# Three phase borders rearranged and the angle products of a random-feature attention stacked to 128 rows

## The reference, cut to what matters

```python
xn = layernorm(x)
x = x + features_attention_and_ffn(xn) + six_local_layers(xn)
xn = layernorm(x)
x = x + linear_attention(xn) + top2_of_8_experts(xn)

def fourier(t, proj):                       # t: 16 heads of 8
    p = einsum('blhd,dm->blhm', t, proj) / sqrt(8)          # the angles, 128 for each head
    return concatenate([cos(p), sin(p)], -1) / sqrt(128)
# attention: kv = einsum('blhm,blhd->bhmd', fourier(k), v); out = einsum('blhm,bhmd->blhd', fourier(q), kv)
# feed-forward of that part: x + relu(ln2(x) @ w1 + b1) @ w2 + b2, w1 128x512, w2 512x128
```

## Time and profile before

| | |
|---|---|
| time, median of 3 runs | 4681.01 us (4677.34 to 4681.03) |
| time of the profiled execution | 4676.1 us |
| its span | 4674.3 us |
| features phase | 0 to 552.4 us of the span |
| layers phase | 552.4 to 4029.5 us |
| experts phase | 4029.5 us to the end |
| busy share of the span | TensorE 93%, DVE 78%, ACT 67%, POOL 38% |

### The profile page before, as it was taken

One profiled execution on the slowest core, in us unless ns is written; L12 is line 12 of the kernel. 1 busy time (PEld: TensorE's weight loads), 2 busy tenths in 40 slices (PEclk: granted clock), 3 DMA queues, 4 the chain that ended last, 5 costly groups with the idle time before them and its releaser, 6 DMA issues. The chain is left out here.

```text
span 4674.3 us, 117986 instructions
## 1 busy us (share of the span) xinstructions
PE 4346.3 (93%) x45025; PEld 3393.8 (73%) x45025; DVE 3656.2 (78%) x6436; ACT 3128.3 (67%) x4910; POOL 1788.8 (38%) x966
## 2 busy tenths in 40 slices
PE   6999589999999999999999999999999999599999
PEld 2333268887788877888778877788878888378878
DVE  6888588888888888888888888888888887555653
ACT  5777367776777767777677776777767777233433
POOL 0000165554555545555455554555545555000000
PEclk9999799999999999999999999999999999789999
DMA  0000122222322323232323223322233322100000
GB/s 29 6 5 5 48 67 68 63 65 59 94 64 63 70 66 81 63 70 67 78 65 70 67 63 79 72 67 64 66 78 72 69 64 67 53 8 7 7 7 5
DMA packets 330938, 254.77 MB, mean 55 GB/s; under 512 B 227224, under 2 KB 231968, under 8 KB 329248
## 3 DMA queue, kind: packets, MB, share of 16 engines
q1 hardware_dynamic: 330400, 247.45, 22.2%
HBM read 29.23 MB, written 4.19 MB: 7 GB/s over the span
## 5 line engine op out<-in xcount | busy, mean ns | idle before, releaser
L672 POOL TENSOR_TENSOR qk_rotated<-qk_rotated,rotary_sines 128x1024 f32<-128x1024 f32 x384 | 923.7, 2405 | 1597.0 <-DVE rotary_sines L759 1597.0
L683 POOL TENSOR_TENSOR qk_rotated<-qk_rotated,rnorm 128x1024 f32<-128x1024 f32 x384 | 733.6, 1911 | 7.4
L767 DVE TENSOR_REDUCE qk_sumsq<-qk_squared 128x16 f32<-128x1024 f32 x384 | 464.9, 1211 | 170.3 <-ACT qk_squared L512 170.2
L519 ACT ACTIVATE q_t<-ps_qk_t 128x512 f32<-128x512 f32 x384 | 229.6, 598 | 456.9 <-PE ps_qk_t L287 456.9
L231 PE MATMUL ps_proj<-qkv_w_hi,x_shifted_hi 128*128 128x512 f32 x1152 | 510.5, 443 | 15.7 <-DVE rotary_sines L759 10.6
L749 DVE TENSOR_TENSOR qk_rotated<-ps_proj,rotary_scaled 128x1024 f32<-128x1024 f32 x384 | 467.7, 1218 | 7.8 <-ACT qk_squared L512 4.6
L759 DVE TENSOR_TENSOR rotary_sines<-ps_proj,rotary_scaled 128x1024 f32<-128x1024 f32 x384 | 466.6, 1215 | 1.7 <-POOL qk_rotated L672 1.7
L233 PE MATMUL ps_proj<-qkv_w_hi,x_shifted_lo 128*128 128x512 f32 x1152 | 459.8, 399 | 0.0
L533 ACT ACTIVATE k_t_by_head<-ps_qk_t 64x512 f32<-64x512 f32 x768 | 452.0, 589 | 11.5 <-PE ps_qk_t L296 2.1
L232 PE MATMUL ps_proj<-qkv_w_lo,x_shifted_hi 128*128 128x512 f32 x1152 | 456.1, 396 | 0.0
L564 ACT ACTIVATE attn_out_t<-ps_attention 128x512 f32<-128x512 f32 x384 | 229.2, 597 | 334.7 <-PE ps_attention L350 334.7
(11 more groups left out here) (247 smaller groups left out, 9528.0 us busy)
## 6 DMA issues: line engine op xcount, KB each, us to landing
v_by_window<-v_tokens SPq DMA_DIRECT2D x1152, 128.0 KB, 2.4
v_by_window<-v_tokens SPq DMA_DIRECT2D x384, 64.0 KB, 2.1
k_t_by_head<-k_t_by_head SPq DMA_DIRECT2D x96, 256.0 KB, 4.3
v_by_window<-v_by_window SPq DMA_DIRECT2D x192, 64.0 KB, 2.0
qkv_w_raw<-in_layer_qk_dram SPq DMA_DIRECT2D x7, 1664.0 KB, 7.8
layer_w<-in_layer_w_dram SPq DMA_DIRECT2D x6, 580.5 KB, 5.7
layer_w<-in_layer_w_dram SPq DMA_DIRECT2D x6, 512.0 KB, 3.7
f_x<-in_x_dram SPq DMA_DIRECT2D x8, 256.0 KB, 5.7
```

The lines of the kernel that those rows point to most:

```text
L672: tt(u, u, TB[:], ALU.add).then_inc(added, 1)
L683: tt(u, u, r.unsqueeze(3).broadcast_to((P, 2, 8, DH)), ALU.mult).then_inc(scaled, 1)
L767: nc.vector.reduce_sum(SS[:, 16 * i:16 * i + 16], SQ[:].rearrange("p (h e) -> p h e", e=DH), AX).then_inc(sumsq, 1)
```

## The change

1. **Stacked angles.** `k_out` and `q_out` now write the high part in fp32r, and a new DVE instruction (`k_low`, `q_low`) writes the rest. SP copies the 32 rows of each head group as high, low, high, low into one stack of 128 rows, 16 transfers for keys and 16 for queries in each block. The projection matrix gets 64 rows of high and 64 rows of low part. An angle product is then one fp32r product of 128 rows. The second norm output of a block (`norm_out(b, 1)`) and what follows from it come some turns earlier. The store of a block stands in SP's program behind the copies of a later one.
2. **Start of the features phase.** TensorE and ACT wait for three small fills only; the clearing of `VP` and `KVP` and the projection's scaling and split come behind the first norm on DVE. ACT computes one sine on a constant first.
3. **Last feed-forward.** In the last block's tail the four hidden products go to four banks, and `tail_out` waits for each relu in turn.
4. **Border to the layers.** The first layer's `RAW` is loaded during the features phase. DVE divides q and k weights before it waits for the tables, and v weights after; TensorE waits for the parts where it uses them. POOL makes the first low part of the input first and then clears `V2`, for which only SP waits. ACT clears `KD`.
5. **Border to the experts.** ACT makes the high part of all the experts' weights during the first attention; DVE makes the low part of two experts before the first turn, and of one more ahead of each expert of the first block.

```diff
@@ layers_phase, SP
-            sp.dma_start(RAW[:], layer_qk[0]).then_inc(raw_in, 16)
...
-            sp.wait_ge(setup, NSETUP)
+            sp.wait_ge(v2_zero, 1)
@@ TensorE
+                pe.wait_ge(split, 2)             # in first(); 4 before k0 and 6 before v0 of turn -1
                 q0(Batch(0, 0))
...
             pe.wait_ge(setup, NSETUP)
-            pe.wait_ge(wo_in, 16)
-            pe.wait_ge(w_in, 16)
-            pe.wait_ge(split, 6)
+            pe.wait_ge(kd_zero, 1)
@@ ACT, first()
                 high_part(Batch(0, 0))
+                act.wait_ge(setup, 2)
+                a(KD[:].rearrange("p h c k -> p (h c) k"), ZS[:, 0:1].unsqueeze(2).broadcast_to((P, 16, KW)), ACT.Copy).then_inc(kd_zero, 1)
+                act.wait_ge(setup, NSETUP)
@@ POOL
                 low_part(Batch(0, 0), (setup, 0))
+                nc.gpsimd.memset(V2[:], 0.0).then_inc(v2_zero, 1)
...
-            nc.gpsimd.memset(V2[:], 0.0).then_inc(setup, 1)
-            nc.gpsimd.memset(KD[:], 0.0).then_inc(setup, 1)
-            pool.wait_ge(setup, NSETUP)
@@ DVE
+            divide(0, 0, proj_v, 0)
+            divide(0, 1, proj_v, 0)
+            dve.wait_ge(const_in, 48)
+            cp(IDR[:], IDENT[:]).then_inc(setup, 1)
+            dve.wait_ge(setup, NSETUP)
             tables(0)
-            for x in range(3):
-                divide(0, x, proj_v, 0)
+            divide(0, 2, proj_v, 0)
@@ features_phase, SP
+            sp.dma_start(RAW[:], qk_first).then_inc(raw_in, 16)
+            def stack(dst, hi, lo, landed):
+                for g in range(4):
+                    rows = slice(32 * g, 32 * g + 32)
+                    for copy in range(2):
+                        sp.dma_start(dst[64 * copy:64 * copy + 32, g, :].bitcast(F32), hi[rows, :].bitcast(F32)).then_inc(landed, 16)
+                        sp.dma_start(dst[64 * copy + 32:64 * copy + 64, g, :].bitcast(F32), lo[rows, :].bitcast(F32)).then_inc(landed, 16)
+            def stack_k(b):
+                sp.wait_ge(kq_hi, 2 * b + 1)
+                sp.wait_ge(kq_lo, 2 * b + 1)
+                if b > 0:
+                    sp.wait_ge(angle, PAIRS * (b - 1) + 8)
+                stack(KST, KHI, KLO, k_in)
...
             for i in range(NBLK):
-                sp.wait_ge(xo, 2 * i + 2)
-                sp.dma_start(x_attn[:, i, :], Y[i % 2][:]).then_inc(x_out[i % 2], 16)
+                stack_k(i)
+                stack_q(i)
+                if i > 1:
+                    store(i - 2)
@@ TensorE, angles(U)
                 if u == 0:
-                    pe.wait_ge(proj_out, 2 * i + 1)
+                    pe.wait_ge(k_in, STACK * (i + 1))
...
-                        last = mm(out, KT[i % 2][rows, c * P:(c + 1) * P], PBF[rows, :], start=True, stop=True)
+                        last = mm(out, KST[:, r, c * P:(c + 1) * P], PST[:], start=True, stop=True)
...
-                        last = mm(out, PBF[rows, j * P:(j + 1) * P], QT[i % 2][rows, :], start=True, stop=True)
+                        last = mm(out, PST[:, j * P:(j + 1) * P], QST[:, r, :], start=True, stop=True)
@@ TensorE and ACT, tail
-                mm(G[:], W[:, A_W1 + k * P:A_W1 + (k + 1) * P], YN[:], start=True, stop=True).then_inc(h_mm, 1)
+                mm(hidden_bank(q, k)[:], W[:, A_W1 + k * P:A_W1 + (k + 1) * P], YN[:], start=True, stop=True).then_inc(h_mm, 1)
@@ DVE, behind the first norm
+            ts(PB[:], PB[:], float(1.0 / (np.sqrt(RD) * 2 * np.pi)), None, ALU.mult).then_inc(setup, 1)
+            dve.wait_ge(setup, 4)
+            cp(PST[:], PB[:]).then_inc(setup, 1)
+            dve.wait_ge(setup, 5)
+            tt(PST[64:P, :], PB[64:P, :], PST[64:P, :].bitcast(F32), ALU.subtract).then_inc(setup, 1)
+            nc.vector.memset(VP[:, 0], 0.0).then_inc(setup, 1)
+            nc.vector.memset(VP[:, 1], 0.0).then_inc(setup, 1)
+            nc.vector.memset(KVP[:], 0.0).then_inc(setup, 1)
+            k_low(0)
+            q_low(0)
...
+                stt(KLO[:], NB[:], vec(AV_BK), KHI[:].bitcast(F32), ALU.add, ALU.subtract).then_inc(kq_lo, 1)
@@ experts_phase
+                if t == 3 and isinstance(i, int) and i == 0:
+                    act.wait_ge(experts_in, 32)
+                    a(WIHI[:], WI[:], ACT.Copy).then_inc(wi_high, 1)
...
+            def w_in_low(e):
+                dve.wait_ge(wi_high, 1)
+                tt(WILO[:, e, :], WI[:, e, :], WIHI[:, e, :].bitcast(F32), ALU.subtract).then_inc(wi_low, 1)
...
-                cp(WIHI[:], WI[:]).then_inc(wi_split, 1)
-                dve.wait_ge(wi_split, 1)
-                tt(WILO[:], WI[:], WIHI[:].bitcast(F32), ALU.subtract).then_inc(wi_split, 1)
```

More of the change, by code:

```diff
@@ L433, in turn @@
                 shift(gs[0])
+                if j == -1:
+                    pe.wait_ge(split, 4)
                 if j == B - 1 and more(layer):
@@ L450, in turn @@
                 k_t(gt[1])
-                if j == 3 and (not isinstance(layer, int) or layer > 0):
+                if j == 3:
                     pe.wait_ge(w_in, layer * 16 + 16)
@@ L466, in turn @@
                 probs_t(gs[2])
+                if j == -1:
+                    pe.wait_ge(split, 6)
                 if j == B - 1 and more(layer):
@@ L1005, in _, with stack_q, store @@
             for i in range(1, NBLK):
-                sp.dma_start(X[:, i, :], xT[:, i, :]).then_inc(x_in[i], 16)
-            for i in range(NBLK):
-                sp.wait_ge(xo, 2 * i + 2)
-                sp.dma_start(x_attn[:, i, :], Y[i % 2][:]).then_inc(x_out[i % 2], 16)
+                sp.dma_start(X[:, i, :], xT[:, i, :]).then_inc(x_in[1], 16)
+            sp.dma_start(RAW[:], qk_first).then_inc(raw_in, 16)
[11 more added lines that the diff above has]
+                stack(KST, KHI, KLO, k_in)
+            def stack_q(b):
+                sp.wait_ge(kq_hi, 2 * b + 2)
+                sp.wait_ge(kq_lo, 2 * b + 2)
+                after(sp, angle, PAIRS * b)
+                stack(QST, QHI, QLO, q_in)
+            def store(q):
+                sp.wait_ge(xo, 2 * q + 2)
+                sp.dma_start(x_attn[:, q, :], Y[q % 2][:]).then_inc(x_out[q % 2], 16)
+            for i in range(NBLK):
+                stack_k(i)
+                stack_q(i)
+                if i > 1:
+                    store(i - 2)
+            store(NBLK - 2)
+            store(NBLK - 1)
             for k in range(2):
@@ L1255, in q_out @@
                 act.wait_ge(proj, 3 * b + 2)
-                after(act, angle, PAIRS * (b - 1))
-                a(QT[b % 2][:], NB[:], ACT.Identity, bias=vec(AV_BQ)).then_inc(proj_out, 1)
+                after(act, q_in, STACK * b)
+                a(QHI[:], NB[:], ACT.Identity, bias=vec(AV_BQ)).then_inc(kq_hi, 1)
             def k_out(b):
                 act.wait_ge(proj, 3 * b + 1)
-                a(KT[b % 2][:], NB[:], ACT.Identity, bias=vec(AV_BK)).then_inc(proj_out, 1)
+                after(act, k_in, STACK * b)
+                a(KHI[:], NB[:], ACT.Identity, bias=vec(AV_BK)).then_inc(kq_hi, 1)
             def kv_scaled(i, s):
@@ L1424, in norm_out, with k_low, q_low @@
                 tt(XF2(XF, b) if k == 0 else X2N[:], ZC[:], NB[:], ALU.mult).then_inc(n_out, 1)
+            def k_low(b):
+                dve.wait_ge(kq_hi, 2 * b + 1)
+                after(dve, k_in, STACK * b)
+                stt(KLO[:], NB[:], vec(AV_BK), KHI[:].bitcast(F32), ALU.add, ALU.subtract).then_inc(kq_lo, 1)
+            def q_low(b):
+                dve.wait_ge(kq_hi, 2 * b + 2)
+                after(dve, q_in, STACK * b)
+                stt(QLO[:], NB[:], vec(AV_BQ), QHI[:].bitcast(F32), ALU.add, ALU.subtract).then_inc(kq_lo, 1)
             def v_out(b):
@@ L1488, in _ @@
                         if u == 7:
+                            norm_out(i + 1, 1)
+                        if u == 8:
                             norm_out(i + 1, 0)
                         if u == 9:
-                            norm_out(i + 1, 1)
+                            k_low(i + 1)
+                        if u == 11:
+                            q_low(i + 1)
                         if u == 13:
@@ L1977, in turn, with first_low @@
                 dve.wait_ge(y_acc, SLOTS * (i + 1))
-            def split_w_in():
-                dve.wait_ge(experts_in, 32)
-                cp(WIHI[:], WI[:]).then_inc(wi_split, 1)
-                dve.wait_ge(wi_split, 1)
-                tt(WILO[:], WI[:], WIHI[:].bitcast(F32), ALU.subtract).then_inc(wi_split, 1)
-            blocks(dve, attention, turn, split_w_in)
+            def first_low():
+                w_in_low(0)
+                w_in_low(1)
+            blocks(dve, attention, turn, first_low)
 HD1 = D // HEADS
```

119 lines of the change are left out of this document (67 added, 52 removed).

## The result

The changed kernel takes 4632.67 us (median of 4 runs, 4630.22 to 4634.77), the kernel before 4681.02 (4 runs, 4677.34 to 4683.21): ratio 0.9900, 95% interval 0.9887 to 0.9913. That is 48.3 us less, and 3.7 more than the 4629 forecast. The profiled execution of after has a span of 4630.4, 43.9 less than before. The rest of the 48.3 is in the medians: the execution profiled before lay 4.9 under its median, this one 0.4.

What follows compares the result with a forecast made beforehand. No engine is full in the feature loop; TensorE's queue is late first. Terms 0 - 30 - 7.5 - 8 - 6.7 took profiled 4676.1 to 4623.9; adding 4.9 for the median gave 4629 us, range 4598 to 4660.

Steps and rivals of the forecast that it cites:

- The loop, -30 forecast: Feature loop: stacked angles shorten TensorE's queue, saving 4.0 us a block over 7.5 blocks; bounds nothing to -57.
- about three pairs lie in TensorE's queue: Feature loop: three ACT waits a block, each behind about three pairs saving 0.6 us, give 5.4 us a block.
- The loop does not gain: Rival, feature loop: late keys or the DVE and ACT ring take the saving; only borders' -22 remain, 4659; chance 0.26.
- The slack: Feature loop: four turns cover the 11.9 us key transfers, so keys land 0.5 us ahead of need.
- DVE's floor: Rival, feature loop: waits fall away almost whole, -57 there and -22 at the borders, 4602 us; chance 0.15.
- The clock: Rival, feature loop: less TensorE work leaves more gaps and low clock, so not faster; 4708 at low-clock share 0.8; chance 0.06.
- The start, 0 forecast: Features phase start: an earlier mean is offset by clears, splits and key stacking before the first angle; bounds -3 to +2.
- The last tail, -7.5: Last feed-forward: with four banks eight products run without a stop, -7.5 us; -2.5 if the clock stays low.
- The layers' border, -8: Features to layers: TensorE starts 11.2 us in, behind the identity's copy held by POOL's V2 fill, for 19.2 before.
- the bound's case: Layers' border: the fill also precedes the k weights' copy; that copy and a subtraction, about 2 us, follow: -6.
- The bound of -13: Layers' border: if the identity's copy precedes POOL's fill, KD on ACT sets TensorE's start at 6 us.
- The experts' border, -6.7: Experts' start: the weights' split moves off TensorE's path, -6.7 us; -2.5 if all six later low parts showed.

Runs made afterwards that it cites:

- e13: The changed kernel with each pair's two angle products issued twice, same result in the same bank; 4636.1 us.
- e11: e5 with the low parts of the keys issued by POOL and the high parts by SP; 4631.7 us.
- e4: The changed kernel with the norm's three diagonal products a block made by POOL, not DVE; 4614.5 us.
- e5: The changed kernel with TensorE's and ACT's norm turns as late as before the change, so keys come two turns later; 4679.5 us.
- e6: The changed kernel with three extra fp32 products a block behind turn 6, result unused; 4624.1 us.
- e3: The changed kernel with the three start clears moved behind the first low parts of keys and queries; ratio 0.9884.
- e12: The changed kernel with low parts of the keys issued by POOL and high parts by SP; 4632.2 us.
- e2: The changed kernel with POOL clearing V2 only after DVE's fifth instruction of the weights' split; 4624.2 us.
- e9: The changed kernel with the edits of e2, e3, e4 and e6 together; 4604.4 us.
- e10: The changed kernel with three extra fp32 products a block at turn 13, ahead of the value projection, result unused; 4644.7 us.

## Why the prediction was right, and where it was not

*The loop, -30 forecast, -21 to -24 measured.* The mechanism was seen rightly as far as it goes: TensorE's queue was late first, the waits for `use` fell by 3.8 a block, and DVE's for the rounding by 5.0. The step that was mis-sized is "about three pairs lie in TensorE's queue between its last idle moment and that `use`: 3 x 3 x 0.6 = 5.4 us". It came out at 21 to 24 for the term of 30, and in the loop the sum has no term at all for the norm's new turns. Here four loops with a pair and an order of turns each:

| loop, us (clock) | the norm as late as before | the changed order |
|---|---|---|
| long pairs | 476.6 (0.92), before | 458.2 (0.97), e13 |
| short pairs | 459.0 (0.93), e11 | 452.8 to 455.6 (0.91 to 0.92), after and its like; 455.3 with e11's two queues |

In these four, either the shorter pair or the earlier norm brings some 18 us; both together bring only 3 to 6 more. So the saving counts until TensorE is no longer late, and then stops; the waits of after say at what: TensorE itself waits 8.4 us a block for DVE's fractions, for 3.7 before. Taking 2.05 us a block off DVE (e4) gave 23 to 25 us, perhaps part of it by the clock, where the shorter pair gave 3 to 5 (after against e13). Two cautions. e11's order is not quite that of before (DVE's `norm_out` is at its new turns and waits 7.1 us there), so with the old order in full the lower left cell may be some us lower. And e13's pair is 0.92 and not 1.06 long, and its products use 128 rows, where those of before use 32; its clock is 0.97 against 0.92, so the upper right cell is not the kernel before with another order, and how much of its 18 is the order and how much the clock stays open; the kernel before with nothing but the new turns was not run.

*The rivals.* "The loop does not gain" was closest to becoming true in another way: with the keys two turns later (e5) all is lost. The slack was forecast at 0.5 us and is 2.7, except behind block 0, where the keys are 2.2 late; that block lasts 51 us for the others' 58, which the forecast left out. "DVE's floor" (4602) was not reached: DVE's busy time is as worked out, 396.8 in the loop, but the loop is 59 longer than that. *The clock* did not turn the change to a loss, but it probably took part of the gain: the place of the earlier trace rows is still there, and filling it (e6) gives 10 to 13. Of the eight us that the prediction calls saturated at 0.50, shows four; the four before them are at 0.60 with TensorE busy 3.57. The rule cited for it (the Trainium skill, TensorE: Matmul & The Clock Gate, HAM oscillation: idle gaps put TensorE back to half clock) bears on what e5 and e6 show, and they agree: TensorE's idle window in e5 is followed by one at 0.50, and in the block of e6 that is shown, where the gap is filled, the clock stays at 1.00.

*The start, 0 forecast, +1.3.* All its parts are there: the mean at 4.00 (10 earlier), the clears ahead of `k_low`, which starts at 27.22, the train of 12. e3 shows the clears are worth 5.2, e12 half a train 5.6.

*The last tail, -7.5 and -8.2.* Right with its mechanism.

*The layers' border, -8 and -7.4.* Right in size, wrong in the instruction. The step was "the identity comes in about 4 us after the border, inside that fill, so the copy ends at" the fill's end. It is the bound's case that came: the fill gets ahead of the copy of the k weights, and the subtraction and the identity's copy follow it. It came out at -7.4 and not at -6 because the fill began 2.8 after the phase's first instruction, for 3.5 forecast, and subtraction and identity's copy behind it took 1.4, for about 2; so TensorE starts 11.8 into the phase, for 11.2 forecast and 13.2 by that bound. The rule named there (the Trainium skill, SBUF — State Buffer, Who interferes with whom) holds in both halves: the cast is held (6.52 for 0.68 without the fill, e2), the subtraction beside the fill is not (1.54, of which 1.0 beside the fill). The bound of -13, for a copy ahead of the fill, is what e2 reaches: 23.2 to 10.0.

*The experts' border, -6.7 and -6.7.* TensorE starts 0.15 behind DVE's last attention instruction, and the later low parts show as 0.4 us.

*The total.* That it is only 3.7 off is in part luck. For the profiled execution the forecast was 4623.9, and it took 4632.2, 8.3 more, most of it the loop's 6 to 9. The 4.9 that the forecast added for the distance between profile and median covers 4.5 of that, because the changed kernel's profiled execution lay only 0.4 under its median.

## What to carry to other kernels

Work taken out of a queue counts only until that queue is no longer the late one; read from the waits which engine is late next, and by how little, before multiplying a saving by its number. A train of small transfers on one queue costs its issues, not its bytes: count issues times pitch (the time from one issue to the next) against the turns that cover them, and split the train over two queues when it stands bare. A gap in which TensorE has almost nothing to do can cost twice, once in length and once in clock behind it; look in the windows for the low busy share ahead of a low clock. But filling a gap need not pay: beside POOL's diagonals the same filling raised the clock and shortened nothing (e9 against e4). And compare windows of two kernels at the same turn of the program, not at the same time: after some blocks they are many us apart.

## What the runs showed of the hardware

- A gap of 4.8 us in TensorE at a block's start was followed by some 6 us at half clock (e5). With the train halved, the waits for keys were some 31 us less in seven blocks and the loop 40.5 less (e5, e11).
- Three products a block whose result nobody uses made the loop shorter by 10 to 13 us at one turn, and longer by 7 to 10 at another (e6, e10).
- Transfers of 64 KB within SBUF are issued at a pitch of 0.63 us by SP and, eight in 4.38 us, of 0.55 by POOL (e11; 0.60 in e12). With both queues at it a transfer landed 2.5 (SP) and 2.3 us (POOL) after its issue, for 2.0 from SP alone (e11, after).
- DVE's cast of 128x1024 took 6.52 us beside POOL's fill and 0.68 without it, while a subtraction of the same size took 1.54, 1.0 of it beside the fill, for 1.22 without (after, e2).
- POOL's product of 128x512 took 1.04 us, DVE's 0.68 (e4, after).
